# The FP4 down product of a two-layer cross-attention and FFN kernel: two fp32r parts and three terms in place of fp32

## What is computed

```python
def fp4_quant_dequant(x):
    xb = x.reshape(shape[:-1] + (shape[-1] // 16, 16))
    scale = jnp.maximum(jnp.max(jnp.abs(xb), axis=-1, keepdims=True) / 6.0, 1e-12)
    xn = xb / scale
    q = _GRID[jnp.searchsorted(_MID, jnp.abs(xn))] * jnp.sign(xn) * scale
...
gate = fp4_linear(x, w_gate)          # 256 -> 704
y = fp4_linear(x, w_up)               # 256 -> 704
h = jax.nn.silu(gate) * y
return fp4_linear(h, w_down)          # 704 -> 256, h is quantized too
```

## Time and profile before

| | |
|---|---|
| median of 3 runs | 1083.4 us (1083.01 to 1083.5) |
| the profiled execution's own time | 1083.78 us |
| its span in the trace | 1081.7 us |
| PE busy, PE weight loads | 983.0 us (91%), 878.6 us (81%) |
| DVE busy | 841.8 us (78%) |
| ACT, POOL busy | 485.0 us (45%), 483.3 us (45%) |

### The profile page before, as it was taken

The page is one execution under the profiler, slowest core; times in us unless marked ns, Lnnn a source line. Parts: engine busy times, 40 slices in busy tenths (PEclk is TensorE's granted clock), DMA queues, the critical chain, the costliest instruction groups (busy, mean ns, idle before and its releaser), DMA issues. The chain is left out here.

```text
span 1081.7 us, 21024 instructions
## 1 busy us (share of the span) xinstructions
PE 983.0 (91%) x6564; PEld 878.6 (81%) x6564; DVE 841.8 (78%) x2047; ACT 485.0 (45%) x1031; POOL 483.3 (45%) x676
## 2 busy tenths in 40 slices
PE   3799999999589999998699999999947999999997
PEld 2699999999578878886589999999945887878785
DVE  5589999998499999986567777777646888888874
ACT  3233333333188888886423232323323444545441
POOL 3234554552266666655211212121116777777662
PEclk8799999999799999999679999999977999999998
DMA  8020000000000000001000000000000000000000
GB/s 332 10 89 1 0 0 1 0 0 1 1 1 1 1 1 0 0 2 47 1 1 2 0 0 0 0 0 0 1 1 2 18 3 20 20 20 21 20 20 20
DMA packets 5350, 17.69 MB, mean 16 GB/s; under 512 B 817, under 2 KB 2225, under 8 KB 4657
## 3 DMA queue, kind: packets, MB, share of 16 engines
q1 hardware_dynamic: 4576, 16.52, 4.0%
q10 hardware_dynamic: 720, 0.50, 0.1%
HBM read 12.83 MB, written 4.19 MB: 16 GB/s over the span
## 5 line engine op out<-in xcount | busy, mean ns | idle before, releaser
L732 ACT COPY a_xTs<-a_psQ 128x256 f32<-128x256 f32 x64 | 23.8, 372 | 299.5 <-PE a_psQ L782 299.5
L774 PE MATMUL a_psS<-kblk,a_qTs 128*128 (+3 forms) x768 | 153.2, 347 | 2.9 <-DVE a_qTs L664 2.9
L1373 PE MATMUL f_psGU<-wgu,f_xTs 128*128 128x512 f32 (+1 forms) x576 | 143.3, 395 | 12.1 <-DVE f_xTs L1157 10.7
L841 PEld LDWEIGHTS a_psO<-vblk,a_prob 128*128 128x128 f32 x1280 | 148.6, 192 | 0.0
L841 PE MATMUL a_psO<-vblk,a_prob 128*128 (+2 forms) x1280 | 148.2, 271 | 0.0
L1373 PEld LDWEIGHTS f_psGU<-wgu,f_xTs 128*128 128x128 f32 x576 | 105.0, 194 | 39.6 <-DVE f_xTs L1157 24.2
L774 PEld LDWEIGHTS a_psS<-kblk,a_qTs 128*128 128x128 f32 x768 | 123.7, 200 | 6.9 <-DVE a_qTs L664 3.4
L610 DVE TENSOR_REDUCE a_mx<-a_psS 128x6 f32<-128x462 f32 (+1 forms) x192 | 109.3, 580 | 20.7 <-PE a_psS L774 17.9
L710 POOL TENSOR_TENSOR a_rstd<-a_mv,expo 128x1 f32<-128x1 f32 x64 | 15.7, 245 | 242.4 <-DVE a_mv L676 242.4
L1044 PEld LDWEIGHTS s_psY<-w,s_hid 128*128 128x128 f32 x768 | 97.5, 188 | 18.2 <-POOL s_hid L962 11.3
L1044 PE MATMUL s_psY<-w,s_hid 128*128 128x256 f32 x768 | 102.3, 282 | 6.9 <-POOL s_hid L962 6.9
(11 more groups left out here) (159 smaller groups left out, 1929.7 us busy)
## 6 DMA issues: line engine op xcount, KB each, us to landing
x<-in_x SPq DMA_DIRECT2D x4, 1024.0 KB, 7.9
out_x<-x SPq DMA_DIRECT2D x8, 512.0 KB, 2.6
w<-in_w SPq DMA_DIRECT2D x1, 2304.0 KB, 8.3
wat<-in_att SPq DMA_DIRECT2D x2, 1024.0 KB, 11.5
w<-in_w SPq DMA_DIRECT2D x2, 1024.0 KB, 13.7
mask<-in_mask SPq DMA_DIRECT2D x4, 308.0 KB, 3.7
rows<-in_rows ACTq DMA_DIRECT2D x1, 384.0 KB, 5.7
ctxT<-in_ctx SPq DMA_DIRECT2D x1, 308.0 KB, 2.9
```

What stands on the lines that cost most here:

```text
L774: mm = nc.tensor.matmul(psS[n][:, (a - h0) * KV:(b - h0) * KV], qTs[:, u, p, k, :], kblk[:, r, t // R, k, (a - 8 * k) * KV:(b - 8 * k) * K ...
L841: mm = nc.tensor.matmul(psO[:, CH[c] * VW:(CH[c] + n) * VW], prob[:, v, c * P:(c + 1) * P], vblk[:, t // R, c * NJ * VW:(c * NJ + n) * VW] ...
L1373: mm = nc.tensor.matmul(psGU[:, n0:n1], xTs[:, u, a, k * P:(k + 1) * P], wgu[:, b, k, n0:n1], start=(n == 0), stop=(n == len(TERMS) - 1))
```

## The change

The down product is made as the gate and up products are: row and weight in two fp32r parts, three terms, 18 products of 256 columns a tile in place of six fp32 ones. `wdT` and `hTs` get a second part. In `second_blocks` VectorE subtracts for three more groups. In `ffn_fp4` VectorE gets two instructions a step, `hT_lower` (512 columns) ahead of `h_exponents` and `hT_lower_rest` (256 columns) ahead of `h_rounded`. TensorE waits for the low parts (`hT_low`) where it waited for the copies.

```diff
-        own(ctx, "wdT", [P, NF1, D])
+        own(ctx, "wdT", [P, 2, NF1, D], F32R)
...
-                           [wdT[:, c:c + 2, :].rearrange("p c n -> p (c n)")], 4 * P))
+                           [wdT[:, part, c:c + 2, :].rearrange("p c n -> p (c n)") for part in range(2)], 4 * P))
...
-                            pe.wait_ge(w_low, min(n - 3, 8))
+                            pe.wait_ge(w_low, n - 3)
...
-                for n, (_, dst, cnt) in enumerate(groups[:2 * B]):
+                for n, (_, dst, cnt) in enumerate(groups):
                     dve.wait_ge(w_copied, n + 1)
                     nc.vector.tensor_tensor(dst[1], psX[n % 4][:, 0:cnt], dst[0].bitcast(F32), ALU.subtract
...
-        hTs = sb("hTs", [P, 2, NF1 * P])
+        hTs = sb("hTs", [P, 2, 2, NF1 * P], F32R)
...
+                def hT_lower(t, u):
+                    wait(dve, hT_copied, 2 * t + 1)
+                    nc.vector.tensor_tensor(hTs[:, u, 1, 0:HTA * P], psA[:], hTs[:, u, 0, 0:HTA * P].bitcast(F32),
+                                            ALU.subtract).then_inc(hT_low, 1)
+
+                def hT_lower_rest(t, u):
+                    wait(dve, hT_copied, 2 * t + 2)
+                    nc.vector.tensor_tensor(hTs[:, u, 1, HTA * P:], psB[:, 0:256], hTs[:, u, 0, HTA * P:].bitcast(F32),
+                                            ALU.subtract).then_inc(hT_low, 1)
...
                         nc.vector.bn_stats(st[:, i % 2, :], x[:, i + 9, :]).then_inc(st_set, 1)
+                    if valid(i - 2):
+                        hT_lower(i - 2, i % 2)
                     if valid(i - 1):
                         h_exponents(i - 1, (i - 1) % 2)
...
                         shifts((i + 5) // SG)
+                    if valid(i - 2):
+                        hT_lower_rest(i - 2, i % 2)
                     if valid(i - 1):
                         h_rounded(i - 1, (i - 1) % 2)
...
-                    nc.scalar.copy(hTs[:, u, 0:HTA * P], psA[:]).then_inc(hT_copied, 1)
+                    nc.scalar.copy(hTs[:, u, 0, 0:HTA * P], psA[:]).then_inc(hT_copied, 1)
...
+                DOWN = [(c, a, b) for c in range(NF1) for a, b in ((1, 0), (0, 1), (0, 0))]
...
-                        wait(pe, hT_copied, 2 * t - 1)
+                        wait(pe, hT_low, 2 * t - 1)
...
-                        wait(pe, hT_copied, 2 * t)
+                        wait(pe, hT_low, 2 * t)
...
-                        wait(pe, hT_copied, 2 * (i - 1))
+                        wait(pe, hT_low, 2 * (i - 1))
...
-                        wait(pe, hT_copied, 2 * t + 1)
-                        for c in range(NF1):
-                            if c == HTA:
-                                wait(pe, hT_copied, 2 * t + 2)
-                            mm = nc.tensor.matmul(psY[:, 0:D], hTs[:, u, c * P:(c + 1) * P], wdT[:, c, :],
-                                                  start=(c == 0), stop=(c == NF1 - 1))
+                        wait(pe, hT_low, 2 * t + 1)
+                        for n, (c, a, b) in enumerate(DOWN):
+                            if n == 3 * HTA:
+                                wait(pe, hT_low, 2 * t + 2)
+                            mm = nc.tensor.matmul(psY[:, 0:D], hTs[:, u, a, c * P:(c + 1) * P], wdT[:, b, c, :],
+                                                  start=(n == 0), stop=(n == len(DOWN) - 1))
```

More of the change, by code:

```diff
@@ L462, in second_blocks @@
             groups.append(([dn[:, j, q * P:(q + 1) * P] for q in (c, c + 1) for j in range(KC)],
-                           [wdT[:, c:c + 2, :].rearrange("p c n -> p (c n)")], 4 * P))
+                           [wdT[:, part, c:c + 2, :].rearrange("p c n -> p (c n)") for part in range(2)], 4 * P))
         order = ([("weights", n) for n in range(2 * B)] + [("mask", 0), ("mask", 1)] +
                  [("weights", n) for n in range(2 * B, len(groups))] + [("mask", 2), ("mask", 3)])
-        assert [len(dst) for _, dst, _ in groups] == [2] * (2 * B) + [1] * (len(groups) - 2 * B)
+        assert [len(dst) for _, dst, _ in groups] == [2] * len(groups)
         with nc.Block() as block:
@@ L1117, in ffn_fp4 @@
             "xT_mm", "xT_high", "xT_low", "gu_mm", "silu_ready", "hid_ready"))
-        hT_mm, hT_copied, y_mm, x_done, stored = (sm(n) for n in ("hT_mm", "hT_copied", "y_mm", "x_done", "stored"))
+        hT_mm, hT_copied, hT_low, y_mm, x_done, stored = (
+            sm(n) for n in ("hT_mm", "hT_copied", "hT_low", "y_mm", "x_done", "stored"))
         FIRST, LAST = -9, T + 3
@@ L1338, in hT_copies @@
                     wait(act, y_mm, t - 1)
-                    nc.scalar.copy(hTs[:, u, 0:HTA * P], psA[:]).then_inc(hT_copied, 1)
+                    nc.scalar.copy(hTs[:, u, 0, 0:HTA * P], psA[:]).then_inc(hT_copied, 1)
                 def hT_rest(t, u):
                     wait(act, hT_mm, 2 * t + 2)
-                    nc.scalar.copy(hTs[:, u, HTA * P:], psB[:, 0:256]).then_inc(hT_copied, 1)
+                    nc.scalar.copy(hTs[:, u, 0, HTA * P:], psB[:, 0:256]).then_inc(hT_copied, 1)
                 def step(i):
```

## The result

| | median us | lowest to highest |
|---|---|---|
| before | 1083.45 | 1083.01 to 1085.58 |
| changed | 1138.55 | 1137.56 to 1139.57 |

The changed kernel is slower: ratio 1.0505, 95% interval 1.0486 to 1.0523. That is 55.1 us. The forecast was 1137. The profiled execution took 1139.03 us with a span of 1136.9 us, 55.2 more than before.

A forecast was written before the change was run, and what follows sets the result against it. VectorE's loop with GpSimd's `h_up` and ScalarE's `h_kick` was taken as the bound, TensorE beside it. Steps 50.4 + 5.2 + 1.6, tail 0.5, less 3.9 hidden, gave 53.8 us: forecast 1137, range 1122 to 1152.

The forecast's parts named there:

- I cost it at nothing: TensorE's down product in `ffn_fp4`: 0.3 us less a tile, worth nothing because TensorE waits for `x_low`.
- start 2.83, `h_exponents` 3.42: Ordinary `ffn_fp4` step, us after `x_low` ends: `hT_lower` starts at 2.83, `h_exponents` at 3.42 instead of 2.33, 1.09 late.
- 1.98 and 2.30 after `h_exponents`: Ordinary `ffn_fp4` step: `hT_lower_rest` starts at 1.98, `h_rounded` at 2.30 instead of 1.45, 0.85 us more.
- the 0.35 us of `shifts` and of GpSimd's power: Two of every four `ffn_fp4` steps: existing delays hidden by longer waits, 11 x 0.35 = 3.9 us given back.
- The sum: Whole kernel: 50.4 + 5.2 + 1.6 + 0.5 - 3.9 = 53.8 us added.
- step 2: `ffn_fp4` step with TensorE at the low clock: `hidden` already waited for TensorE, so only 1.6 us more.
- steps 3 to 28: Ordinary `ffn_fp4` steps: 26 x 1.94 = 50.4 us more, before the 3.9 us given back.
- the last three: `ffn_fp4` steps 29 to 31, no `x_lowered` ahead of the second copy: 3 x 1.72 = 5.2 us more.
- what follows the last `h_largest`: Tail of `ffn_fp4`: eighteen products take 4.2 us against 4.97, subtractions add 0.62 and 0.7; together 0.5 us more.
- this rival: `ffn_fp4`: TensorE's idle times lower its clock; 1186 us if always low, 1153 if in a third of steps; 8%.
- Only VectorE's work counts: `ffn_fp4`: waits cost nothing, only 0.33 us a step is added; 10 us, 1094 in all; 5%.
- TensorE is the bound: `ffn_fp4`: TensorE's 0.3 us less a tile makes the kernel faster, 1073.4 us; 3%.

The follow-up runs named there:

- e3: Changed kernel without both hidden-row subtractions, eighteen fp32r products reading only the high part, TensorE waiting for the copies: 1084.27 us against 1085.61 before.
- e6: Changed kernel without both hidden-row subtractions, only twelve fp32r products a tile (row's high part by both weight parts): 1084.72 us against 1084.12 before.
- e10: Kernel with the order of e8 on all engines, but the twelve-product down product of e6, no hidden-row subtraction: 1079.63 us against 1085.19 before.
- e8: Kernel before, hidden-row transposes ahead of first products, second hT copy ahead of `h_kick`, `x_low` behind `h_inverse`: 1078.98 us against 1084.12.
- e1: Changed kernel with `hT_lower` moved from ahead of `h_exponents` to behind `shifts`, all work kept: 1109.12 us against 1085.61 before.
- e4: Changed kernel with both subtractions and all waits, but six fp32 down products a tile from the high parts: 1138.39 us against 1085.61 before.
- e7: Changed kernel, all three terms, hidden-row transposes ahead of TensorE's first products, second hT copy ahead of `h_kick`: 1090.95 us against 1084.12 before.
- e2: Changed kernel with `hT_lower_rest` moved between two halves of a split `h_rounded`, `hT_lower` unmoved: 1121.44 us against 1084.12 before.
- e5: Changed kernel with both subtractions cut to 8 columns, waits kept, all eighteen products reading the row's high part: 1113.60 us against 1085.61 before.

## Why the prediction was right

**Which loop.** TensorE at 97% busy was off the path. e3, e6 and e10 take 0.4 to 1.1 us of TensorE's work a tile away, and the ordinary step stays where it was: 7.64 us in e3 and e6 as in the kernel before, 7.60 in e10 against 7.59 in e8. That was "I cost it at nothing". Of the price of eighteen products, the 2.45 us that I took measured 2.37.

**`hT_lower`.** Forecast: start 2.83, `h_exponents` 3.42. Measured 2.81 and 3.42. The price was 0.692 us where I took 0.68; the slope of the rows that write fp32r had given 0.69. The idle time of 0.84 us at that place was no cover, since what the instruction waits for comes at 2.78. e1 shows it: work unmoved in amount, wait gone.

**`hT_lower_rest`.** Forecast 1.98 and 2.30 after `h_exponents`, measured 1.96 and 2.30. The step: 9.58 forecast, 9.57 to 9.58 measured, all alike, so that the 0.35 us of `shifts` and of GpSimd's power did vanish behind the longer waits.

**The sum, stretch by stretch.** Between the `h_largest` of the two kernels step 2 is 1.64 us longer (forecast 1.6), steps 3 to 28 together 46.6 (forecast 50.4 - 3.9 = 46.5), each of the last three 1.72 (as forecast), and what follows the last `h_largest` 0.5 (as forecast). So no term was far off and made good by another.

**The small terms.** In `second_blocks` the last subtraction ended before VectorE's next work began. That work starts 0.64 us after TensorE's first product for it in both kernels (525.26 and 525.90 before, 526.65 and 527.29 now), so this part cost nothing:

```profile
526.56 0.69 DVE L527 TENSOR_TENSOR wdT<-m_psX,wdT 128x512 fp32r<-128x512 f32 x1 [0.16 <-ACT wdT L511]
...
527.29 0.80 DVE L247 TENSOR_TENSOR vblk<-m_psV,blockmask 128x192 f32<-128x192 f32 x2
```

The last product took 4.20 us at the low clock, as forecast:

```profile
1129.26 4.20 PE f_psY L1435 x18
```

**The remainder.** The sum was 53.8 and the spans differ by 55.2. In this execution `ffn_fp4` began 1.3 us later than in that of before (GpSimd's first power for `rstd` at 804.51, not 803.23), which leaves 53.9. The delay was there before `second_blocks`: the first product of 256 columns in `ffn_sine` starts at 308.95 us, not at 307.42. Over the runs of this study the first `x_low` of `ffn_fp4` started between 812.2 and 814.8 us, whatever the kernel, so I count it as scatter of the earlier stages. The cause of it stays open. The price itself scatters as much: 55.1 us here and 52.8 for e4, on either side of the forecast.

**The rivals.** From step 3 to the tail (840 to 1116 us) the clock of the changed kernel stayed at 1.00, the level of 2.4 GHz, with two idle times of 1.1 us in 9.6. The Trainium skill (TensorE: Matmul & The Clock Gate, A second HAM failure mode: psum-queue depth-cycling) tells of a clock that goes back and forth for idle times between groups; the changed kernel doesn't show it in this stretch. e6 and e10 do: with less work for TensorE, the granted clock fell in three of their steps (0.62 over 880 to 884 us in e6, 0.57 over 972 to 976 us in e10), and these took 1.0 to 1.4 us more. So the loss that this rival feared can come in this stage; 1.1 us of idle time twice a step didn't bring it in the changed kernel, and no run shows what does. "Only VectorE's work counts" would have been 1094. e7 comes near it, 1090.95, once most of the waiting is taken away: the mechanism exists, and it needed another order on two other engines. "TensorE is the bound" is excluded by the steps of e3 and e6. The Trainium skill's count of four passes for fp32 (FP8 and Floating Point Precision, TensorE Precision Notes) would, as an estimate, have had three terms take 2.07 of 2.76 us; they took 2.37.

## What to carry to other kernels

Before you give a waiting instruction to the engine that sets the loop, ask when its input lands, counted from the loop's own clock. Idle time ahead of a place is no cover for an instruction whose input comes after that idle time: here 1.1 us of work a step cost 1.94, and with the same work placed behind its input, or the input made earlier, 0.86 and 0.33. A busy share of 97% on an engine that idles once a step for another one's result says nothing about what less work for it would bring; cut its work and see, before building on it. Look at the steps then, and not only at the total: in e6 a gain at the end of the stage and two steps at a lower clock cancelled. When work is moved to fit a tight engine, look for pairs in which one instruction needs the result of the one just ahead: what is put between them is partly free, and what is taken out from between them gives little back.

## What was not expected of the hardware

In this stage VectorE lost time between neighbours of which one needs the other's result. The two halves of `h_rounded` start 0.92 us apart with nothing between them and 1.13 apart with 0.41 us of other work between them (e2). `h_scale` on 44 columns lasts 0.33 us directly behind the reduction that it reads (e8) and 0.17 with `x_low` between, in the kernel before. So 0.41 us of independent work cost 0.2 us in the one place and 0.05 in the other, while ahead of `h_rounded` in the changed kernel the same work came to its length less 0.08. In each such pair the second instruction also waits for a semaphore of the first, so these runs don't tell whether the data or the semaphore costs the time.

The recorded length of the same instruction depends on its place. The subtraction of 512 columns took 691 to 692 ns in all 32 steps of the changed kernel, where it always waited for its copy. In e1, where the copy had landed in most steps, it took 628 to 693 ns, 654 in the median. `x_low` took 0.41 us behind `h_largest` and 0.36 behind `h_inverse` (e8). Cut to 8 columns the first subtraction still lasted 166 ns (e5).

The clock fell where TensorE had less to do. Of the five idle times of 1.80 us ahead of e6's first products two were followed by steps at a lower clock, which took 8.64 and 8.66 us in place of 7.64; the changed kernel, with 1.13 and 1.14 us idle in each step, kept 1.00.
